# The chain between two attentions by 512-token halves, with one root chain for layer norm and rms norm

## The reference, cut to what matters

```
x = layernorm(x + attention0(x))            # 8 heads of 16, causal, plus a rank-one term per head
x = layernorm(x + ffn(x)), where ffn is:
    h = rmsnorm(x) * norm1_w
    q = rope(h @ Wq.T)
    latent = layernorm(h @ Wdkv.T) * ln_g + ln_b      # 64 columns
    k = rope(latent @ Wuk.T);  v = latent @ Wuv.T
    x = x + softmax(causal(q k / sqrt(8))) v @ Wo.T   # 16 heads of 8
    x = x + mixture of 4 experts (rmsnorm(x) * norm2_w), one expert per token
```

## Time and profile before

| what | value |
|---|---|
| profiled execution, device time | 684.45 us |
| its span, first to last instruction | 682.7 us |
| median of three runs | 679.21 us |
| mean granted TensorE clock | 0.932 of full |
| TensorE matmul busy | 604.6 us (89%) |
| VectorE busy | 412.7 us (60%) |
| ScalarE busy | 338.0 us (50%) |
| GpSimd busy | 144.0 us (21%) |
| chain that ended last | TensorE 67%, VectorE 19%, DMA 4%, ScalarE 3% |

### The profile page before, as it was taken

How to read it: one execution, slowest core, us unless ns; L and a number is a source line. 1 busy time by engine, 2 the same in 40 slices (tenths; PEclk the granted TensorE clock), 3 DMA queues, 4 the chain that set the end, 5 groups by cost and what they waited for, 6 DMA issues and landing times.

```text
span 682.7 us, 10113 instructions
## 1 busy us (share of the span) xinstructions
PE 604.6 (89%) x3694; PEld 282.8 (41%) x3717; DVE 412.7 (60%) x1031; ACT 338.0 (50%) x621; POOL 144.0 (21%) x180
## 2 busy tenths in 40 slices
PE   5578899958798878889999999999989999899994
PEld 3323233424233224333433344455544555357663
DVE  3586988795603967897778787845657401422313
ACT  4234457634445434546766666645546554633330
POOL 3812212312344022125330202211002001101000
PEclk9889999968658998999999999999999999989998
DMA  4855120000035121031231221030000000000000
GB/s 142 205 175 186 33 75 22 2 1 0 28 75 96 21 43 22 1 64 45 63 49 32 33 45 21 17 48 1 2 0 17 0 2 1 17 0 1 16 1 15
DMA packets 27394, 27.69 MB, mean 41 GB/s; under 512 B 6289, under 2 KB 22545, under 8 KB 27090
## 3 DMA queue, kind: packets, MB, share of 16 engines
q1 hardware_dynamic: 26962, 26.26, 16.2%
q0 software_dynamic: 384, 0.79, 0.5%
HBM read 19.40 MB, written 7.34 MB: 39 GB/s over the span
## 4 chain that ended last, share of the span: by engine, by line
PE 67%; DVE 19%; DMA 4%; ACT 3%; issue 3%; POOL 1%; SPq 1%; DVEq 0%; ACTq 0%; POOLq 0%
PE ps L863 14%; PE ps L846 12%; PE ps L936 10%; DVE mparts L1225 10%; PE ps L823 9%; PE ps L992 8%; PE ps L925 3%; PE ps L919 3%; PE ps L820 2%; ACT pr L1012 2%; PE ps L900 2%; PE ps L874 2%; PE ps L934 2%; DMA qs<-nparts 1%; DVE stats L1135 1%
## 5 line engine op out<-in xcount | busy, mean ns | idle before, releaser
L1012 ACT ACTIVATE pr<-ps 128x512 f32<-128x512 f32 (+1 forms) x456 | 250.6, 576 | 239.3 <-PE ps L846 236.6
L1225 DVE TENSOR_REDUCE mparts<-ps 128x1 f32<-128x512 f32 (+3 forms) x456 | 280.0, 656 | 116.1 <-PE ps L823 114.9
L846 PE MATMUL ps<-qs,ks 99*128 99x512 bf16 (+3 forms) x576 | 174.6, 344 | 12.0 <-ACT pr L1012 6.0
L823 PE MATMUL ps<-ks,qs 96*128 96x512 bf16 (+3 forms) x576 | 170.8, 338 | 15.6 <-DVE mparts L1225 12.7
L740 POOL TENSOR_SCALAR_AFFINE_SELECT pr<-pr 128x512 f32<-128x512 f32 x96 | 60.9, 635 | 370.4 <-ACT pr L1012 370.2
L863 PE MATMUL ps<-pr,vs 128*32 128x512 f32 (+3 forms) x1152 | 131.3, 530 | 0.0
L846 PEld LDWEIGHTS ps<-qs,ks 99*128 99x128 bf16 x576 | 51.0, 100 | 148.6 <-ACT pr L1012 83.9
L823 PEld LDWEIGHTS ps<-ks,qs 96*128 96x128 bf16 x576 | 55.7, 101 | 54.0 <-DVE mparts L1225 21.2
L936 PE MATMUL ps<-w,work 128*128 128x128 f32 x512 | 74.1, 288 | 0.0
L820 PE MATMUL ps<-cmask,identb 128*128 128x128 bf16 (+2 forms) x241 | 58.0, 241 | 17.3 <-DVE mparts L1225 8.9
L1077 ACT ACTIVATE work<-ps,b 128x512 f32<-128x512 f32 x64 | 43.8, 687 | 49.1 <-PE ps L992 48.4
(11 more groups left out here) (115 smaller groups left out, 400.0 us busy)
## 6 DMA issues: line engine op xcount, KB each, us to landing
qs<-scr1q SPq DMA_DIRECT2D x64, 64.0 KB
ks<-scr1k SPq DMA_DIRECT2D x64, 64.0 KB
qs<-scr0q SPq DMA_DIRECT2D x48, 64.0 KB, 2.3
ks<-scr0k SPq DMA_DIRECT2D x36, 64.0 KB, 2.2
scr0q<-parts SPq DMA_DIRECT2D x4, 384.0 KB, 2.9
scr0k<-parts SPq DMA_DIRECT2D x4, 384.0 KB, 3.2
scr1q<-parts SPq DMA_DIRECT2D x4, 384.0 KB, 2.5
scr1k<-parts SPq DMA_DIRECT2D x4, 384.0 KB, 2.5
```

The source lines that it names most:

```text
L823: last = pe.matmul(bank[:, h, :], queries(F, KMAX, h0 + h, i * P, P), ks[0:KMAX, F % SLOTS, h0 + h, 512 * c:512 * c + w], start=not diagon ...
L846: last = pe.matmul(to[:, h, :], ks[0:KEXP, F % SLOTS, h0 + h, j * P:(j + 1) * P], queries(F, KEXP, h0 + h, qb * 512 + lo, n), start=True, ...
L1012: act.activation(pr[:, st % PSLOTS, h0:h0 + nh, 0:STEPS[st][3]], scores_at(F, v), ACT.Exp, scale=GROUPS[F][0].scale).then_inc(exped, 1)
L1225: dve.tensor_reduce(mparts[:, F % SLOTS, h0:h0 + nh, i, c], maxes_at(F, u), AX_X, ALU.max).then_inc(taken, 1)
```

## The change

`between` now takes a batch and a half and is spread four times instead of two: batch 0 at 1.56 to 2.15 and 2.22 to 2.82, batch 1 at 3.56 to 4.2 and 4.22 to 5.2. The root chain x1 computes two rows at once: 1/sqrt(var + 1e-5) and, from the same variance, the product of the layer norm's and the rms norm's factor. `square`, `square_sum`, `root rms0` and `hat` of the first kind go. Instead VectorE writes the doubly normed values (`hat0`) into x0 and GpSimd writes x1. The latent root chain runs per half. Group 4's q and k are loaded by halves. The maxima of group 4 are spread from 2.98 to 3.84. The loads of group 5 stand at 2.82.

```diff
+HALVED = range(ATT[0].groups + 1)
...
 def split_block(M):
-    return (n, b, M // 2 % 2, M % 2) if n else (n, b, M % 2, M // 2 % 2)
+    return n, b, M % 2, M // 2 % 2
...
-MAX_LATE = (0.4, 0.9)
+MAX_LATE = (-0.02, 0.84)
...
+def between(b, i):
+
+    q = block_of(1, b, 0, i)
+    k = block_of(1, b, 1, i)
+    latent = root("latent", b, (i,))
+    return [*output(0, b, (i,)), ("moments", 0, b, i), *root("x1", b, (i,)), ("hat0", b, i), ("x1", b, i),
+            ("feed", "hat0", b, i), ("feat", "hat0", b, i),
+            ("latent", b, i), ("lat_copy", b, i), ("proj", q, 0), ("lat_moments", b, i), ("rotate", q, 0),
+            ("proj", q, 1), *latent[:2], ("rotate", q, 1), *latent[2:], ("rotated", q), ("lat_norm", b, i), ("hi", q),
+            ("lat_turn", b, i), ("r1", q), ("lat_feat", b, i), ("mid", q), ("proj", k, 0), ("lo", q),
+            ("rotate", k, 0), ("store", q), ("proj", k, 1), ("rotate", k, 1), ("rotated", k),
+            ("v_proj", 1, b, i), ("hi", k), ("v_out", 1, b, i), ("r1", k), ("mid", k), ("lo", k), ("store", k)]
...
-LONG = {"layer_norm": 1.5, "hat": 2.0, "lat_norm": 2.0, "moments": 1.5, "pick": 1.5}
+LONG = {"layer_norm": 1.5, "hat": 2.0, "hat0": 1.5, "lat_norm": 2.0, "moments": 1.5, "pick": 1.5}
...
 def loads(position, F):
-    if F >= ATT[0].groups:
+    if F not in HALVED:
         return [(position, ("load", F, k, 2)) for k in range(2)]
     return [(position, ("load", F, k, i)) for i in range(2) for k in range(2)]
...
-    out += spread(between(0), *BETWEEN[0]) + loads(BETWEEN[0][1], 4)[1:] + loads(BETWEEN[0][1], 5)
-    out += spread(between(1), *BETWEEN[1])
+    first = loads(0, ATT[0].groups)
+    for i in range(2):
+        out += spread(between(0, i), *BETWEEN[0][i]) + [(BETWEEN[0][i][1], step) for _, step in first[2 * i:2 * i + 2]]
+        out += spread(between(1, i), *BETWEEN[1][i])
+    out += loads(BETWEEN[0][1][1], ATT[0].groups + 1)
...
-BETWEEN = [(2.21, 3.12), (4.21, 5.95)]
+BETWEEN = [[(1.56, 2.15), (2.22, 2.82)], [(3.56, 4.2), (4.22, 5.2)]]
...
+                elif kind == "x1":
+                    b, i = args
+                    pool.wait_ge(done["root"], nth("root", "x1", b, (i,), 3))
+                    for t in range(TB * b + 4 * i, TB * b + 4 * i + 4):
+                        last = pool.tensor_scalar(x1[:, t, :], xn[:, t, :], mv[:, t, 0:1], rstd[:, 2, t:t + 1],
+                                                  ALU.subtract, ALU.mult)
+                    last.then_inc(done["x1"], 1)
...
+                rows = {"x1": slice(0, 2), "result": slice(0, 1), "latent": slice(1, 2), "rms1": slice(1, 2)}[of]
+                v, y, h = (rstd[:, rows.start + k:rows.stop + k, t] for k in (0, 2, 4))
...
+                        if of == "x1":
+                            link(dve.tensor_scalar(rstd[:, 1, t], mv[:, t, 1], 1.0 + RMS_EPS, LN_EPS * RMS_EPS, ALU.mult, ALU.add))
+                        link(dve.tensor_scalar(rstd[:, 0, t], mv[:, t, 1], 1.0, LN_EPS, ALU.mult, ALU.add))
...
                     dve.wait_ge(done["y"], nth("y", n, b, i))
+                    if n == 1:
+                        dve.wait_ge(done["x1"], nth("x1", b, i))
...
+                elif kind == "hat0":
+                    b, i = args
+                    dve.wait_ge(done["root"], nth("root", "x1", b, (i,), 3))
+                    for t in range(TB * b + 4 * i, TB * b + 4 * i + 4):
+                        last = dve.tensor_scalar(x0[:, t, :], xn[:, t, :], mv[:, t, 0:1],
+                                                 rstd[:, 3, t:t + 1], ALU.subtract, ALU.mult)
+                    last.then_inc(done["hat0"], 1)
```

More of the change, by code:

```diff
@@ L248, in root, with rms @@
     return [("root", of, b, blocks, part) for part in range(4)]
-def rms(n, b, blocks):
-    out = [("square", n, b, i) for i in blocks] + [("square_sum", n, b, i) for i in blocks]
-    out += root(f"rms{n}", b, blocks) + [("hat", n, b, i) for i in blocks]
+def rms(b, blocks):
+    out = [("square", b, i) for i in blocks] + [("square_sum", b, i) for i in blocks]
+    out += root("rms1", b, blocks) + [("hat", b, i) for i in blocks]
     for i in blocks:
-        if n:
-            out.append(("x12", b, i))
-        out += [("feed", f"hat{n}", b, i), ("feat", f"hat{n}", b, i)]
+        out += [("x12", b, i), ("feed", "hat1", b, i), ("feat", "hat1", b, i)]
     return out
@@ L269, in output @@
     return out
[L272 to L303, removed]
-    out += block(M0 + 2) + block(M0 + 3)
-    v = []
-    for i in range(2):
-        v += [("v_proj", 1, b, i), ("v_out", 1, b, i)]
-    last = tail.pop(M0 + 3)
-    for k in range(5):
-        out += [last[k]] + v[k:k + 1]
-    return out
+def between(b, i):
[9 more added lines that the diff above has]
+            ("v_proj", 1, b, i), ("hi", k), ("v_out", 1, b, i), ("r1", k), ("mid", k), ("lo", k), ("store", k)]
 def ready(b, blocks):
-    out = output(1, b, blocks) + rms(1, b, blocks)
+    out = output(1, b, blocks) + rms(b, blocks)
     for i in blocks:
@@ L893, in feed @@
                     tile = [att[:, 4 * i + t, b * C:(b + 1) * C] for t in range(4)]
+                elif src == "hat0":
+                    pe.wait_ge(done["hat0"], nth("hat0", b, i))
+                    tile = [x0[:, TB * b + 4 * i + t, :] for t in range(4)]
                 else:
-                    pe.wait_ge(done["hat"], nth("hat", int(src[3]), b, i))
+                    pe.wait_ge(done["hat"], nth("hat", b, i))
                     tile = [xn[:, TB * b + 4 * i + t, :] for t in range(4)]
@@ L1282, in _ @@
                     t0 = TB * b + 4 * i
-                    moments(lambda t: lat[:, t - TB * b, :], range(t0, t0 + 4)).then_inc(done["lat_moments"], 1)
+                    moments(lambda t: lat[:, t - TB * b, :], lat_mv, range(t0, t0 + 4)).then_inc(done["lat_moments"], 1)
                 elif kind == "lat_norm":
                     b, i = args
-                    dve.wait_ge(done["root"], nth("root", "latent", b, (0, 1), 3))
+                    dve.wait_ge(done["root"], nth("root", "latent", b, (i,), 3))
                     for t in range(4 * i, 4 * i + 4):
-                        last = dve.tensor_scalar(lat[:, t, :], lat[:, t, :], mv[:, TB * b + t, 0:1],
-                                                 rstd[:, 1, TB * b + t:TB * b + t + 1], ALU.subtract, ALU.mult)
+                        last = dve.tensor_scalar(lat[:, t, :], lat[:, t, :], lat_mv[:, TB * b + t, 0:1],
+                                                 rstd[:, 3, TB * b + t:TB * b + t + 1], ALU.subtract, ALU.mult)
                     last.then_inc(done["lat_norm"], 1)
```

69 lines of the change are left out of this document (33 added, 36 removed).

## The result

The changed kernel takes 726.94 us (median of 4 runs, 723.77 to 731.95) where the kernel before takes 682.43 in the same comparison (676.43 to 690.13): a ratio of 1.069, 95% interval 1.057 to 1.081. It is 45 us slower; the prediction was 667. The profiled execution took 723.77, its span is 722.0, and the mean granted clock fell from 0.932 to 0.908.

The account below looks back on a forecast made before the run. Plain groups are bound by TensorE at full clock; groups 1 to 5 also lose 49.1 us idle or at half clock. 156.5 + 40 + 24 (four S) + 13 (R) = 233.5 against 245.6, a 12 us gain: 667, range 658 to 679.

Parts of the forecast that it names:

- S: TensorE time lost per half chain, two stalls plus half clock behind them: 7.0 us in batch 0, 5 in batch 1.
- R: TensorE gap at group 3, its rows queued behind group 5's loads: 11 us plus 2 of half clock, 13.
- 196.5: TensorE work in groups 1 to 5: five plain groups, 156.5 us, plus the chain's own matmuls, 40.
- The idle spots under the root chains: Two TensorE stalls in each half, while VectorE runs the x1 and then the latent root chain: 3 to 5 us each.
- first stalls: TensorE idle from y to the feed of hat0 in a half: 4.8 us, scaled to 3.6, in batch 0.
- second ones: TensorE idle from latent to lat_turn in a half: 2.4 us, scaled to 1.8, in batch 0.
- Scaling by three quarters: Stall sums cut by three quarters, because the same sum for the old batch 0 gave 11 us against 8.3 measured.
- the clock behind them: Half clock after stalls: 3 us at 1.2 GHz per half, 1.6 lost, since maxima run beside the chain almost everywhere.
- Rival 4: Each half falls to 1.2 GHz and stays there through its k projections: 16 us slower, 695; chance 0.18.
- 49.1 us beyond work: TensorE idle or half-clock time in groups 1 to 5 before: 40.5 us in batch 0, 8.6 in batch 1.
- x1 on GpSimd: Four operations per half, without a row: 1.5 us taken, between bounds 1.04 and 4.2; nothing on the path.
- Root chains: Small VectorE operations per batch: 50 for 36, 0.2 us apart, so 2.8 us more of VectorE.

Follow-up runs that it names:

- b1: a1 with 14 unused matmuls before each TensorE wait for hat0 and lat_norm in all four halves: 695.31 us (ratio 1.018).
- a3: Kernel before with only the fused root chain, hat0 on VectorE and x1 on GpSimd; whole batches, old positions, loads and maxima: 666.68 us (0.984).
- a2: Changed kernel with only group 5's loads moved back to 3.02, behind the rows of group 3: 716.56 us (1.058).
- a1: Changed kernel with group 4's second-half loads and group 5's loads both moved behind the rows of group 3: 711.19 us (1.050).
- e1: a1 with x1 on GpSimd moved to the end of each half's list: 718.17 us (1.050).
- f1: a3 with the maxima of group 4 spread from 3.3 to 3.92 instead of 3.4 to 3.9: 667.92 us (0.977).
- d5: a1 with batch 1's two halves given more room, 3.56 to 4.6 and 4.62 to 5.95: 690.57 us (1.012).
- c1: a3 with 12 more small VectorE operations in each x1 and each latent root chain, 48 in all: 678.47 us (0.993).
- d1: a1 with all four halves spread wide and overlapping, loads and maxima of group 4 and loads of group 5 moved to suit: 698.34 us (1.024).
- e3: a1 without the Newton steps of the x1 and latent root chains, 72 small VectorE operations less: 682.60 us (1.000).

## Why the prediction was wrong, point by point

The forecast was 4S + R = 37 above 196.5; measured are 284.9 - 196.5 = 88.4. In the terms above these are 16.2 (rows), 22.0 (under the root chains), 32.3 (slow clock) and 17.9 (58.4 - 16.2 - 22.0, less 0.46 in each plain group). Forecast were 11, 17.6, 8.4 and nothing.

- **The idle spots under the root chains: near in the sum, not in the parts.** I gave 3.6 and 1.8 us to a half of batch 0 and 3.4 to one of batch 1, 17.6 in all; 22.0 came. Batch 0 had 17.4 for 10.8: its first stalls took 4.2 and 4.1, its second ones 4.7 and 4.5, more than twice my 1.8. Scaling by three quarters, fitted to the chain before, made both too small. Batch 1 had 4.6 for 6.8.
- **The failed step is the clock behind them.** "I take 3 us at half clock per half, 1.6 lost", and 2 behind the rows: 8.4. Measured 32.3. b1 shows the cause, since the same kernel with the rows first and the stalls filled loses 1.8, where without the filling it loses 28.9. The reason given, that maxima beside the chain keep TensorE active, was an argument without a row; from 252 to 256.7 and from 269.0 to 276.3 maxima were part of what TensorE waited for (2.5 and 1.5 us), and 10 and 24 us at half clock came with it. The rows against it were in hand: 178 to 204.5, busy and slow.
- **Rival 4** was nearest with 695, at 0.18, but not by its own sign. It had the half clock stay through the k projections, with pairs of 2.0 us in three or more halves. One half of four had them (2.07, from 279.1 and 285.1), the others took 1.12. It was the q projections, right behind the stalls for `hat0`, that ran slow: five of eight pairs took 1.75 to 1.91.
- **Small waits set to nothing.** I let all 49.1 us beyond work go and put back only S and R. But 17.9 of other waits stayed, 10.3 of them for the maxima, against 15.1 before. a3 has 17.2 such (25.9 less 3.0, 3.4 for the rows and the plain 2.3), so they come without halves too. This is the second failed step, 18 us.
- **R: the order right, what held the queue not, size 16.2 for 11.** The rows did stand behind group 5's loads. Group 4's second-half loads, placed earlier at 2.82 and waiting for a `store` of k that comes at 204.24, stood there as well: 32 copies, not 16. I had priced these at nothing ("where nothing needs it"). And I had SyncE wait there for the last scores of group 2; it waited for the k of the chain instead, and from 204.24 on it issued without a pause. By the medians group 5's loads cost 10.4 us (after to a2) and group 4's 5.4 (a2 to a1).
- **x1 on GpSimd:** 13.1 us for 16, 0.82 each or 3.3 for four, where I took 1.5 between 1.04 and 4.2. Moving it off the stall (e1) won nothing.
- **Root chains:** 50 operations for 36 was right, and so was 0.2 each where GpSimd is quiet. That a half's chain is almost as long as a batch's was missed in its effect: the operations do not shrink with the columns, so each half of batch 0 has 25 of them within 0.6 of a group.
- **The shapes:** groups near 44, 53, 55, 48, 34 were forecast; 55.5, 75.3, 56.1, 64.6, 33.4 came. The gap before group 3 lies in the 75.3 of group 2, and group 4 stood at a mean clock of 0.74. Group 4's 3.4 us wait for rows is gone, as said; groups from 6 on are unchanged, so the frame held.
- **The part that was good** went unpriced as such: the fused chain with fewer operations over whole batches gives 0.984 (0.974 to 0.994) in a3 and 0.977 in f1. Both are below the kernel before clear of noise, neither by a sure 2%, and far below the changed one.

Accounted for: from a3 to a1, 41.3 us over the five groups, are 19.2 under the root chains and 22.9 of slow clock, less 0.8 elsewhere. From a1 to after, 17.5 are 14.1 idle and 3.4 slow clock. Two things stay open. One is why the clock stays at 1.2 GHz for a few, 10 or 24 us of mostly busy work; no run changed that alone, and in one and the same stretch of schedule it was a few us in a1 and 20 in d5. The other is how the 60 us of halving divide between more small operations, two chains in a row and less room for each: c1, d5, d1 and e3 each show that their part counts, not how much of the 60 it is.

## What to carry to other kernels

Cutting a serial chain in two halves the wide operations and doubles the narrow ones, and two chains in a row share the room that one had. Before splitting, work out how long each part's chain still is, and ask what TensorE has in its list for that long. The narrow operations alone were cheap where they were covered (c1) and dear where they were not (e3). Price each new stall of TensorE, and each run of short waits, with the clock behind it, by the rows that show how long it lasted in this kernel; here that was as much again as the stall and more, and it varied from one profile to the next. A load moved ahead in a queue must be read with everything that waits in front of the next urgent transfer, the loads that wait for a late store included.

## What the runs showed of the hardware

- A TensorE stall of 4.1 us, up to 171.6, brought some 10 us at 1.2 GHz (170.0 to 180.1: busy 8.47 of 10.10 at 0.50). So did a run of waits of 1.2 to 1.3 us each (busy 1.04 of 4.70 from 252.0 to 256.7, and 9.10 of 10.30 at 0.50 from 255.2); another such run (busy 3.66 of 7.30 from 269.0 to 276.3) stands at the start of 24 us (272.0 to 296.2). Unused matmuls in the stalls kept the clock at 0.94 and 1.00 in groups 1 and 2 (b1), where it was 0.85 and 0.89 without them (a1).
- The same schedule at the same point, behind the same stall, had the full clock back after a few us in one profile (a1, 0.92 from 191 to 212) and not for 20 us in another (d5, 0.51).
- A VectorE operation with two SBUF inputs and 4 columns waited for a GpSimd operation to end: 1.26 us for 0.17. In d1 four `tensor_scalar` took 3.31 us (VectorE's row first; 0.98 for four at 140.67 in the kernel after). The first of them took 2.08 and ended at 146.0, as a memset of GpSimd did (second row, to 145.9):

```profile
143.91 3.31 DVE L1286 TENSOR_SCALAR work<-work,lat_mv,rstd 128x64 f32<-128x64 f32 x4
```
```profile
142.44 3.50 POOL L702 MEMSET qs<- 32x4096 bf16 x1
```

- A rows transfer behind 32 load copies landed 5.44 us after its issue, against 1.83 where the queue had issued nothing for 29 us before it.
